# The order of waits in a recurrent kernel: which signal rides on the operation

## The reference

```python
# layer 0: GRU over time, state h [4, 512]
r = sigmoid(i_r + h_r); z = sigmoid(i_z + h_z)
n = tanh(i_n + r * h_n)                  # gi = x_t @ W_ih + b_ih, gh = h @ W_hh + b_hh
h = (1.0 - z) * n + z * h
x = x + h
# layer 1: four stages of a Runge-Kutta step, states q, p [4, 512]
dq = q - q**3 / 3.0 - p + drive_t + tanh(q) @ coupling.T + bias
dp = EPSILON * (q + ALPHA - BETA * p)
q_next = clip(q + DT / 6.0 * (dq1 + 2*dq2 + 2*dq3 + dq4)); p_next likewise
x = x + q_next
# layer 2: block attention pooled to one vector a sample, projection, layer norm
# layer 3: linear interpolation of x along the features at a grid
```

## Time and profile before

| | before |
|---|---|
| median of 3 runs | 3659.87 us (3658.0 to 3660.68) |
| the profiled execution | 3661.45 us, its span 3659.7 us |
| granted TensorE clock, mean of the span | 0.989 |
| PE busy | 3546.2 us (97%) |
| DVE busy | 2998.4 us (82%) |
| ACT busy | 2574.2 us (70%) |
| POOL busy | 1507.0 us (41%) |
| DMA | mean 7 GB/s |

### The profile page before, as it was taken

The page is one execution under the profiler, slowest core; times in us unless marked ns, Lnnn a source line. Parts: engine busy times, 40 slices in busy tenths (PEclk is TensorE's granted clock), DMA queues, the critical chain, the costliest instruction groups (busy, mean ns, idle before and its releaser), DMA issues.

```text
span 3659.7 us, 298613 instructions
## 1 busy us (share of the span) xinstructions
PE 3546.2 (97%) x115469; PEld 3220.4 (88%) x115469; DVE 2998.4 (82%) x20699; ACT 2574.2 (70%) x22689; POOL 1507.0 (41%) x6169
## 2 busy tenths in 40 slices
PE   8989999999999999999999999999999999999978
PEld 4479999999999999999999999999999999999954
DVE  2078888888888888888888888888888888888876
ACT  3257777777777777777777777777777777777753
POOL 0034444444444444444444444444444444444421
PEclk9999999999999999999999999999999999999978
DMA  3000000000000000000000000000000000000001
GB/s 127 23 25 1 1 1 1 1 1 1 1 1 1 1 1 1 1 1 1 1 1 1 1 1 1 1 1 1 1 1 1 1 1 1 1 1 1 1 2 46
DMA packets 9454, 24.45 MB, mean 7 GB/s; under 512 B 557, under 2 KB 601, under 8 KB 8793
## 3 DMA queue, kind: packets, MB, share of 16 engines
q1 hardware_dynamic: 8832, 19.92, 1.5%
q10 hardware_dynamic: 88, 0.02, 0.0%
HBM read 15.75 MB, written 4.19 MB: 5 GB/s over the span
## 4 chain that ended last, share of the span: by engine, by line
PE 79%; DVE 14%; issue 4%; ACT 3%; DVEq 0%; DMA 0%; ACTq 0%; POOL 0%; POOLq 0%
PE psum L1180 43%; PE psum L1138 29%; PE psum L1108 5%; DVE psum L887 2%; DVE tpart L843 2%; DVE gates L776 2%; ACT tpart L571 1%; PE psum L1283 1%; DVE psum L878 1%; DVE psum L866 1%; DVE fresh L795 1%; DVE narg L787 1%; DVE hs L812 1%; ACT tfull L573 1%; DVE hpart L819 0%
## 5 line engine op out<-in xcount | busy, mean ns | idle before, releaser
L1180 PE MATMUL psum<-tpart,cpl 128*128 128x32 f16 x65536 | 1995.8, 177 | 34.1 <-DVE tpart L843 15.0
L1180 PEld LDWEIGHTS psum<-tpart,cpl 128*128 128x128 f16 x65536 | 1788.7, 96 | 150.9 <-DVE tpart L843 41.5
L1138 PE MATMUL psum<-hpart,whh 128*128 128x32 f16 x49152 | 1622.9, 176 | 28.8 <-DVE hpart L819 24.4
L1138 PEld LDWEIGHTS psum<-hpart,whh 128*128 128x128 f16 x49152 | 1404.1, 96 | 91.5 <-DVE hpart L819 30.4
L843 DVE SCALAR_TENSOR_TENSOR tpart<-tfull,tpart 128x8 f16<-128x8 f32 x4096 | 668.4, 163 | 146.6 <-ACT tfull L573 9.9
L571 ACT ACTIVATE tpart<-psum 128x8 f16<-128x8 f32 x3072 | 544.0, 177 | 245.8 <-DVE psum L887 177.2
L887 DVE TENSOR_REDUCE psum<-psum 128x8 f32<-128x24 f32 x3072 | 585.5, 192 | 133.9 <-PE psum L1180 12.2
L573 ACT ACTIVATE tfull<-psum 128x8 f32<-128x8 f32 x3072 | 529.2, 172 | 0.0
L571 ACT ACTIVATE tpart<-qnext 128x8 f16<-128x8 f32 x1024 | 213.9, 209 | 434.6 <-DVE qnext L887 434.5
L535 ACT ACTIVATE qterm<-psum 128x16 f32<-128x16 f32 x3072 | 400.6, 184 | 111.0 <-DVE psum L866 109.1
L374 POOL TENSOR_TENSOR kept<-rz,hs 128x8 f32<-128x8 f32 x1024 | 209.2, 204 | 466.5 <-ACT rz L500 465.6
(11 more groups left out here) (152 smaller groups left out, 4040.5 us busy)
## 6 DMA issues: line engine op xcount, KB each, us to landing
xrow<-in_x_dram SPq DMA_DIRECT2D x4, 1024.0 KB, 11.3
out_dram<-space SPq DMA_DIRECT2D x16, 256.0 KB, 2.0
wih<-in_L_cond_W_ih_dram SPq DMA_DIRECT2D x3, 1024.0 KB, 9.6
space<-in_L_cond_W_hh_dram SPq DMA_DIRECT2D x1, 3072.0 KB, 18.6
space<-in_L_cond_coupling_dram SPq DMA_DIRECT2D x1, 1024.0 KB, 19.2
xrow<-in_cond_dram SPq DMA_DIRECT2D x1, 1024.0 KB, 4.7
wih<-in_L_cond_Wk_dram SPq DMA_DIRECT2D x1, 1024.0 KB, 5.6
wih<-in_L_cond_Wo_dram SPq DMA_DIRECT2D x1, 1024.0 KB, 8.0
```

The source lines that it names most:

```text
L1138: mm = pe.matmul(gate_out[x][:, :, :, c * B:(c + 1) * B], whh[:, w, k, n * P:(n + 1) * P], copies_in(hpart[:, k, :, :]), start=(c == 0 and ...
L1180: mm = pe.matmul(stage_out[a][:, :, :, col:col + B], cpl[:, w, k, n * P:(n + 1) * P], copies_in(tpart[:, s % 2, k, :, :]), start=(col == 0 ...
```

## The change

Where an operation has several waits, their order changes, and some are left out. In `first_drive` phat_ready is now first; in `plain_h` hs_ready[1] is first and the wait for x1_ready stays for v = 2 and 3 alone; in `sum_gates`, `weigh`, `new_high`, `h_low` and `sum_stage` the order is turned (gate_mm, cand_ready, fresh_ready, hs_ready, stage_mm first); in `sum_stage` half b no more waits for base_ready; in `clip` the waits for q1plain_ready and qterm_ready[0] are gone. No operation is moved, added or removed.

```diff
             def first_drive(v):
 
+                pool.wait_ge(phat_ready, v)
                 pool.wait_ge(uhat_ready, v)
-                pool.wait_ge(phat_ready, v)
                 pool.tensor_tensor(drive0[:, :], uhat[:, :], phat[:, :], ALU.subtract).then_inc(drive0_ready, 1)
...
             def plain_h(v):
 
-                for x in range(HALVES):
-                    act.wait_ge(hs_ready[x], v)
-                if v > 1:
+                act.wait_ge(hs_ready[1], v)
+                act.wait_ge(hs_ready[0], v)
+                if v in (2, 3):
                     act.wait_ge(x1_ready, v - 1)
...
             def sum_gates(x, v):
 
+                dve.wait_ge(gate_mm[x], v)
                 if x == 0:
                     dve.wait_ge(gibase_ready, v)
-                dve.wait_ge(gate_mm[x], v)
...
             def weigh(x, v):
 
+                dve.wait_ge(cand_ready[x], v)
                 dve.wait_ge(omz_ready[x], v)
-                dve.wait_ge(cand_ready[x], v)
...
             def new_high(x, v):
 
+                dve.wait_ge(fresh_ready[x], v)
                 dve.wait_ge(kept_ready[x], v)
-                dve.wait_ge(fresh_ready[x], v)
                 if v < T:
                     if x == 0:
                         dve.wait_ge(ka_read, v)
...
             def h_low(x, v):
 
-                dve.wait_ge(hi_ready[x], v + 1)
                 if v > 0:
                     dve.wait_ge(hs_ready[x], v)
+                dve.wait_ge(hi_ready[x], v + 1)
...
             def sum_stage(s, a, v):
 
-                dve.wait_ge(base_ready, stage_count(s, v))
                 dve.wait_ge(stage_mm[s][a], v)
-                if a == 0 and s in (1, 2):
-                    dve.wait_ge(qterm_ready[s], v)
+                if a == 0:
+                    dve.wait_ge(base_ready, stage_count(s, v))
+                    if s in (1, 2):
+                        dve.wait_ge(qterm_ready[s], v)
...
             def clip(v):
 
                 dve.wait_ge(stage_sum[3][1], v)
-                if v > 1:
-                    dve.wait_ge(q1plain_ready, v - 1)
-                dve.wait_ge(qterm_ready[0], v)
```

## The result

| | before | after |
|---|---|---|
| median | 3660.27 us | 3535.28 us (3533.48 to 3537.49) |
| ratio | 1 | 0.9659, 95% interval 0.9643 to 0.9676 |
| the profiled execution's span | 3659.7 us | 3535.7 us |
| busy: PE, DVE, ACT | 3546.2, 2998.4, 2574.2 us | 3437.3, 2882.1, 2539.2 us |

The change takes 125 us away, 3.4%.

The account below looks back on a forecast made before the run. PE carries 79% of the chain but idles 0.47 us a step for operands from DVE and ACT. Links of -0.185 and stalls of +0.02 make -0.165 us a step, -84 us: 3577 us from 3661.45, range 3540 to 3630.

Parts of the forecast that it names:

- The price of a wait: On DVE, a late signal costs some 0.07 us more on a separate wait than on a riding one.
- Links 1, 2, 4, 5, 8 and 9: In order: sum_stage(0, a) -0.01 or +0.06; sum_gates(a) -0.01; weigh(a) -0.08; new_high(a) -0.01; new_high(b), base(3) -0.08; sum_stage(3, a) +0.07 us.
- link 9: sum_stage(3, a): base comes last and goes from a riding to a separate wait, +0.07 us a step.
- rival A: Slower: base late on a separate wait in stages 0, 2 and 3, +0.16 us a step, 3743 us; chance 0.07.
- links 7 and 8: weigh(b), where cand now rides, -0.08 us; new_high(b) then base(3), where L878 starts earlier, -0.08 us.
- Link 6: argument(b) and what follows: L787 and L506 move up against each other, -0.02 us a step.
- Off this chain: Half b's sums, stage 2's half a sum, h_low, clip, first_drive and plain_h: not on the chain, 0 us.
- The correction for stalls: DVE stalls 8% rarer, but those hidden behind PE will show: +0.02 us a step, bounds -0.01 and +0.07.
- The clip: Loses a pair of waits of 50 ns ahead of L897, not on the chain: 0, at best -0.05 us.
- B: No difference, 3661 us: the operation, not the wait's kind, sets starts, or PE's products set the step; chance 0.06.
- C: Half the gain, 3619 us: DVE's or ACT's limits replace waits in weigh, or stalls reach their upper bound; chance 0.18.
- D: More gain, 3528 us: stage 0's base early in all steps (-0.22), clip on chain (-0.03), rarer stalls (-0.01); chance 0.07.

Follow-up runs that it names:

- the GRU's waits alone: The kernel before with the new waits of weigh, new_high and h_low alone: 3571.03 us, ratio 0.9751.

## Why the prediction was wrong in size

- **What bounds the kernel, and how long the new chain is without PE:** right in the main. DVE and ACT are now most of the chain, L795 and L805 moved as told, base and the sums of stages 0 and 3 stand 0.11 apart, and the sum of stage 1 stayed 0.12 behind L535's signal. "PE is not in it" was too much: the sums of half b start on the products' signal in every stage, and PE keeps 30% of the page's chain.
- **The price of a wait, 0.11 against 0.04:** right, seen at every place, with 0.09 for the second of a pair.
- **Links 1, 2, 4, 5, 8 and 9:** right, each within 0.01 us on the mean of 502 steps. That base goes on a separate wait (link 9) costs 0.07 as told, and rival A fell because L878 comes 0.17 earlier by links 7 and 8 (the table), where 0.07 was enough. Link 6 gave nothing: L787's end and L506's start are 0.05 apart before and after, so that links 6 and 7 together make -0.074 where I had -0.10.
- **The step that failed: "Off this chain".** I put the four sums of half b at nothing, because PE takes half a first. The chain doesn't pass to the next stage over PE alone: it goes through ACT and DVE, each of which works in one order, and in that order the square of stage 3, L866, L787 and L506 stand behind operations of half b, whose sums wait for PE's products of half b. Undone, half b costs 70 us. A part of that was in my sum unseen, since "links not named keep their length" needs half b to keep up with half a; the part not in it is the -0.037 and -0.027 of the table, of which 0.014 in the second, which the run on half b did not give back, stays open.
- **The correction for stalls, +0.02:** wrong in sign. The stalls take 51.0 us before and 40.8 after, -0.020 us a step; I had argued that stalls hidden by PE would show.
- **The account:** forecast -0.185 us a step for the links and +0.02 for stalls, -0.165. Measured on the mean of 502 steps: -0.240, stalls included. Of the 0.055 between this and -0.185 the two missed stretches make 0.064, link 6 takes 0.026 back, and the small misses of the others give the rest. The other 0.02 is the correction. Of the -0.240, -0.020 is in stalls, so that the links by themselves made some -0.22.
- **The clip:** put at nothing ("at best -0.05"). It makes 0.027 us in its stretch and 0.015 in the step, 4 us in time, not told from nothing. It stands in the same stretch as half b of stage 3, which by itself makes 0.060 there; the two cover each other, so their shares of the -0.037 can't be told apart.
- **The rivals:** B (waits are free) fell: the GRU's waits alone, with not one operation or wait fewer, make 2.5%. With it falls, for late signals, the rule weighed in the prediction (the Trainium skill's page "VectorE: DVE Perf Modes", "The DRAIN you can't avoid"); for early signals the run with eight more waits goes most of the way with it. C (half of the gain) fell. D, under 3545 us with a chance of 0.07, is where the time fell, and its -0.26 a step and 3528 us were nearest, but in part by luck. Of its three reasons the rarer stalls hold (-0.020 where it had -0.01), the clip holds at most in part, and the first is wrong: stage 0's base isn't early enough in all steps, its link became longer by 0.025 on the mean. Half b, which made up for that, is not among them.

## What to carry to other kernels

Only the wait that is written first rides on its operation; give that place to the signal that comes last by the trace, at each place on its own: the same line wanted the products in half b, qterm in stage 1 and base in the others, and that order gave 0.9% more than one order for all (0.15% of it, not told from nothing, in stage 3). Where several engines work each in one order, follow the chain through everything that stands ahead in these orders, the other half's operations too, before a term is put at nothing. Read a link's length over all steps of a trace before it is called typical: the one step shown here has the clip at 0.01 and stage 0 at -0.01, where the means are 0.027 and +0.025. And test the parts of such a change together as well as one by one: 0.07% and 2.49% made 3.41%.

## What the runs showed of the hardware that I had not expected

- A separate wait whose signal is long there is nearly free: 4094 of 21 ns cost 10 us.
- What they cost is in stalls of DVE, most of them 128 instructions of its queue apart or a multiple of that: 40.8 us of them at 17 separate waits a step, 51.7 at 25.
- DVE's operations make up for a part of a small delay: on the mean of 502 steps the clip's pair of waits set the second L843 back by 0.044 us, L853 by 0.034 and L860 by 0.027.
